# Expert rows scaled by slot and scatter-added to x1 in DRAM, with eight scan units after the last expert tile

## What is computed

```
x1  = x  + attention(layernorm(x), ctx)
x2  = x1 + moe16(layernorm(x1))          # 16 experts of width 192, top 2 per token, SiLU
x3  = x2 + mamba(ctx, layernorm(x2))     # state-space scan over 512 positions, 16 states, 512 channels
out = x3 + moe8(layernorm(x3))           # 2 of 8 experts of width 2048, GELU, chosen for all tokens
```

## Time and profile before

| | |
|---|---|
| time, median of 3 runs | 1595.75 us (1594.79 to 1597.31) |
| the profiled execution, first to last instruction | 1594.7 us |
| the median less that span | 1.05 us |
| PE busy, share of the span | 1391.5 us, 87% |
| DVE | 936.9 us, 59% |
| ACT | 709.8 us, 45% |
| POOL | 784.0 us, 49% |

### The profile page before, as it was taken

One profiled execution on the slowest core, in us unless ns is written; L12 is line 12 of the kernel. 1 busy time (PEld: TensorE's weight loads), 2 busy tenths in 40 slices (PEclk: granted clock), 3 DMA queues, 4 the chain that ended last, 5 costly groups with the idle time before them and its releaser, 6 DMA issues.

```text
span 1594.7 us, 18873 instructions
## 1 busy us (share of the span) xinstructions
PE 1391.5 (87%) x6080; PEld 1030.4 (65%) x6080; DVE 936.9 (59%) x1186; ACT 709.8 (45%) x1303; POOL 784.0 (49%) x607
## 2 busy tenths in 40 slices
PE   6988983588899989897166999999999999999998
PEld 3535532566666656664166787878787887878786
DVE  2677767999999999998683224241414224241413
ACT  4445433266766776665143333333333333333332
POOL 0000000788888988885631445444544545444442
PEclk9898895699999999999555999999999999999999
DMA  3202214477977987863655900010000100010000
GB/s 105 108 26 81 107 53 165 158 240 257 315 257 234 319 269 264 281 198 125 218 198 203 364 14 0 0 66 1 14 0 13 52 13 0 0 53 0 0 0 26
DMA packets 78202, 191.29 MB, mean 120 GB/s; under 512 B 10856, under 2 KB 15752, under 8 KB 77120
## 3 DMA queue, kind: packets, MB, share of 16 engines
q1 hardware_dynamic: 64832, 157.03, 29.3%
q0 software_dynamic: 6400, 20.98, 4.1%
q10 hardware_dynamic: 6912, 12.59, 2.2%
HBM read 152.55 MB, written 38.01 MB: 119 GB/s over the span
## 4 chain that ended last, share of the span: by engine, by line
PE 58%; DVE 22%; issue 10%; ACT 4%; POOL 3%; DMA 3%; ACTq 0%; SPq 0%; DVEq 0%; POOLq 0%
PE decay L1675 22%; PE bank L1664 21%; DVE decay L1247 11%; DVE S L1256 4%; PE bank L1474 2%; PE decay L1430 2%; PE bank L1437 1%; DVE XH L1114 1%; PE bank L1494 1%; PE bank L1534 1%; PE decay L1484 1%; PE bank L1619 1%; POOL Y L767 1%; PE bank L1561 1%; PE decay L1480 1%
## 5 line engine op out<-in xcount | busy, mean ns | idle before, releaser
L1387 DVE CAST HFH<-HF 128x512 fp32r<-128x512 f32 x128 | 59.0, 461 | 496.7 <-ACT HF L1045 496.7
L815 POOL TENSOR_TENSOR W2L<-W2R,W2H 128x512 fp32r<-128x512 f32 x128 | 172.5, 1347 | 348.2 <-ACT W2H L1040 348.2
L728 POOL TENSOR_TENSOR S<-DTU,Bb 128x1024 f32<-128x1024 f32 x128 | 304.7, 2401 | 25.1 <-DVE row_hot L1229 21.7
L1247 DVE TENSOR_TENSOR_SCAN decay<-decay,S 128x1024 f32<-128x1024 f32 x128 | 292.9, 2288 | 0.5 <-ACT decay L892 0.5
L1664 PE MATMUL bank<-XSH,W1H 128*128 128x512 f32 x512 | 202.9, 396 | 4.2 <-POOL W1L L811 4.2
L1675 PE MATMUL decay<-W2H,HFH 128*128 128x512 f32 x512 | 200.4, 391 | 5.3 <-DVE HFL L1389 5.3
L1664 PE MATMUL bank<-XSH,W1L 128*128 128x512 f32 x512 | 203.0, 396 | 0.0
L1664 PE MATMUL bank<-XSL,W1H 128*128 128x512 f32 x512 | 202.3, 395 | 0.0
L1675 PE MATMUL decay<-W2L,HFH 128*128 128x512 f32 x512 | 199.9, 390 | 0.0
L1675 PE MATMUL decay<-W2H,HFL 128*128 128x512 f32 x512 | 199.7, 390 | 0.0
L811 POOL TENSOR_TENSOR W1L<-W1R,W1H 128x512 fp32r<-128x512 f32 x128 | 171.1, 1337 | 49.6 <-ACT W1H L1031 49.6
(11 more groups left out here) (212 smaller groups left out, 2102.3 us busy)
## 6 DMA issues: line engine op xcount, KB each, us to landing
WGU<-in_L_ffn_gate_w SPq DMA_DIRECT2D x48, 384.0 KB, 3.8
WGU<-in_L_ffn_up_w SPq DMA_DIRECT2D x48, 384.0 KB, 5.1
WD<-in_L_ffn_down_w SPq DMA_DIRECT2D x48, 384.0 KB, 4.9
Bb<-bc_rows SPq DMA_DIRECT2D x32, 512.0 KB, 7.9
Cb<-bc_rows SPq DMA_DIRECT2D x32, 512.0 KB, 9.7
expert_rows<-YT ACTq DMA_DIRECT2D x48, 256.0 KB, 4.2
W1R<-in_L_ffn_w SPq DMA_DIRECT2D x6, 1024.0 KB, 13.9
W2R<-in_L_ffn_w SPq DMA_DIRECT2D x6, 1024.0 KB, 14.1
```

The lines of the kernel that those rows point to most:

```text
L728: pool.tensor_tensor(S[u % NP][:], DTU[:, ds(b, 1), c, :].to_broadcast([P, PAIR, L]), Bb[j][:], ALU.mult).then_inc(dbu_ready, 1)
L815: pool.tensor_tensor(W2L[f % 2][:], W2R[:, ds(e, 1), f, :].rearrange("p e d -> p (e d)"), W2H[f % 2][:].bitcast(F32), ALU.subtract).then_i ...
L1247: dve.tensor_tensor_scan(flat, flat, S[u % NP][:].rearrange("p i l -> p (i l)"), 0.0, ALU.mult, ALU.add).then_inc(scan_done, 1)
```

## The change

- The table by tile gets a second half: for each of the 32 pairs (choice k, token column) there are now two instructions of 48 elements, one with the token number plus 1, one with the routing weight. The contraction on TensorE has 96 columns in place of 48. VectorE then makes `slot_w` (half the weight of the slot), `slot_tok` and `slot_dst` (the token, or one of 128 spare rows where a slot is empty).
- `x1` is stored to `x2_rows` in DRAM. `copy_y` scales by the slot's weight into one of two `YT` buffers, and GpSimd adds the 128 rows onto `x2_rows` by an indirect DMA with an addition (`add_rows`). Each of these waits for the landing of the one before. ScalarE's store, all `gather_y`, `load_x1`, `add_first`, `add_second` and the copy to `gcol` are gone.
- 112 units are dealt over the tiles, and eight (`TAIL`) follow the last tile. The last two `add_rows` stand between these.
- SP loads `x2` for all four batches when the last addition has landed; X2 has four buffers. Three of the eight C buffers are loaded only after the routing, because the new table lies in their place.

```diff
-PAD = 6200
+PAD = 14200
+TAIL = 8
+LATE = 5
...
-        cuts = [AHEAD + (ALL - AHEAD) * j // SLOT_TILES for j in range(SLOT_TILES + 1)]
+        cuts = [AHEAD + (ALL - AHEAD - TAIL) * j // SLOT_TILES for j in range(SLOT_TILES + 1)] + [ALL]
...
-            sp.wait_ge(yt_stored, SLOT_TILES * DMA + DMA)
+            sp.wait_ge(yt_added, SLOT_TILES * DMA)
             sp.sem_inc(xt3_stored, DMA)
-            load_x1(0)
-            load_x1(1)
+            for b in range(B):
+                load_x2(b)
...
                 pool.wait_ge(xgt_ready, j + 1)
-                pool.tensor_copy(gcol[n % 2][:], slot_tok[:, ds(j, 1)]).then_inc(gcol_ready, 1)
-                wait_apart(pool, gcol_ready, j + 1)
                 pool.indirect_dma_start(out=XG[n % 2][:], out_offset=None, in_=xn_dram,
...
+            def add_rows(j):
+
+                pool.wait_ge(yt_ready, j + 2)
+                if j:
+                    pool.wait_ge(yt_added, j * DMA)
+                pool.indirect_dma_start(out=x2_rows, out_offset=bass.IndirectOffsetOnAxis(ap=slot_dst[:, j:j + 1], axis=0),
+                                        in_=YT[j % 2][:], in_offset=None, compute_op=ALU.add).then_inc(yt_added, DMA)
...
                 gate_by_up(j)
+                if j >= 2:
+                    add_rows(j - 2)
                 if j + 2 < SLOT_TILES:
                     gather(0, j + 2)
...
+            last = units(SLOT_TILES)
+            for u in last[:2]:
+                dbu(*bu(u))
+            add_rows(SLOT_TILES - 2)
+            dbu(*bu(last[2]))
+            add_rows(SLOT_TILES - 1)
+            for u in last[3:]:
+                dbu(*bu(u))
...
             for k in range(TOP):
-                ins = dve.tensor_tensor(
-                    tile_hot[:, k], iota_j[:].rearrange("p (o j) -> p o j", o=1).to_broadcast([P, NT, SLOT_TILES]),
-                    jf[:, k, :].rearrange("p (t o) -> p t o", o=1).to_broadcast([P, NT, SLOT_TILES]), ALU.is_equal)
-            do(ins)
-            for k in range(TOP):
-                dve.tensor_tensor(
-                    tile_hot[:, k], tile_hot[:, k], tokid[:].rearrange("p (t o) -> p t o", o=1).to_broadcast([P, NT, SLOT_TILES]),
-                    ALU.mult).then_inc(hot_ready, 1)
+                for t in range(NT):
+                    dve.tensor_scalar(tile_hot[:, k, t, 0, :], iota_j[:], jf[:, k, t:t + 1], tokid[:, t:t + 1],
+                                      ALU.is_equal, ALU.mult)
+                    ins = dve.tensor_scalar(tile_hot[:, k, t, 1, :], iota_j[:], jf[:, k, t:t + 1], rwt[:, k, t:t + 1],
+                                            ALU.is_equal, ALU.mult)
+            ins.then_inc(hot_ready, 1)
+            do(dve.tensor_scalar(spare_row[:], tokid[:, 0:1], float(B * L - 1), None, ALU.add))
...
-                    dve.tensor_copy(slot_tok[:], TURN[:, 0:SLOT_TILES]).then_inc(slots_ready, 1)
+                    ids = TURN[:, 0:SLOT_TILES]
+                    dve.tensor_scalar(slot_w[:], TURN[:, SLOT_TILES:2 * SLOT_TILES], 0.5, None, ALU.mult)
+                    dve.tensor_scalar(empty[:], ids, 0.0, spare_row[:], ALU.is_equal, ALU.mult)
+                    do(dve.tensor_scalar(tokf[:], ids, -1.0, 0.0, ALU.add, ALU.max))
+                    dve.tensor_copy(slot_tok[:], tokf[:])
+                    do(dve.tensor_tensor(empty[:], empty[:], tokf[:], ALU.add))
+                    dve.tensor_copy(slot_dst[:], empty[:]).then_inc(slots_ready, 1)
...
-            add_first(0)
-            add_second(0)
-            add_first(1)
+            for u in units(SLOT_TILES):
+                scan(*bu(u))
+                read_out(*bu(u))
+            statistics_x2(0)
+            statistics_x2(1)
```

More of the change, by code:

```diff
@@ L240, in build_program @@
         XT3 = sb(g, "XT3", [P, K, L])
+        logits = sb(g, "logits", [P, NT, E2])
         vare3 = sb(g, "vare3", [P, T])
@@ L366, in build_program @@
         yt_ready = sem("yt_ready")
[L367 to L373, removed]
+        yt_added = sem("yt_added")
+        spare_set = sem("spare_set")
+        x2_loaded = [sem(f"x2_loaded{b}") for b in range(B)]
         var2_ready = sem("var2_ready")
@@ L453, in build_program @@
         ALL = B * UB
-        cuts = [AHEAD + (ALL - AHEAD) * j // SLOT_TILES for j in range(SLOT_TILES + 1)]
+        cuts = [AHEAD + (ALL - AHEAD - TAIL) * j // SLOT_TILES for j in range(SLOT_TILES + 1)] + [ALL]
+        assert TAIL <= UB // 2
         def units(j):
-            return list(range(HP, AHEAD)) if j < 0 else list(range(cuts[j], cuts[j + 1])) if j < SLOT_TILES else []
+            return list(range(HP, AHEAD)) if j < 0 else list(range(cuts[j], cuts[j + 1])) if j <= SLOT_TILES else []
         def split(j):
@@ L502, in sequence_transfers @@
                     load_x(b + 1)
[L503 removed]
+                sp.dma_start(x2_rows[ds(b * L, L), :].rearrange("(t p) d -> p t d", p=P), X1A[:]).then_inc(x1_stored, DMA)
                 sp.wait_ge(xd_copied, b + 1)
@@ L510, in _ @@
             load_x(0)
+            sp.dma_start(x2_rows[B * L:B * L + P, :], x[0, 0:P, :]).then_inc(spare_set, DMA)
             for stored in (u_spilled, bc_stored, x1_stored, xn1_stored):
@@ L587, in _ @@
             load_down(0)
+            for j in range(LATE, NP):
+                load_c(0, j)
             load_gate_up(1)
@@ L951, in _ @@
             act.sem_inc(yt_ready, 1)
-            act.sem_inc(yt_stored, DMA)
             copy_xg(0, 0)
@@ L980, in _ @@
             copy_y(0, SLOT_TILES - 1)
-            store_y(0, SLOT_TILES - 1)
-            for u in units(SLOT_TILES - 2)[-1:] + units(SLOT_TILES - 1):
-                if u % HP == HP - 1:
-                    take(u)
+            before = units(SLOT_TILES - 2)[-1:] + units(SLOT_TILES - 1)
+            for u in units(SLOT_TILES):
+                if u != units(SLOT_TILES)[0]:
+                    decay(*bu(u))
+                for v in before:
+                    if v % HP == HP - 1:
+                        take(v)
+                before = [u]
+            take(ALL - 1)
             def silu_z(b):
@@ L1603, in _ @@
                 down(0, j)
-            for u in units(SLOT_TILES - 1):
+            for u in units(SLOT_TILES - 1) + units(SLOT_TILES):
                 add_states(*bu(u))
```

138 lines of the change are left out of this document (47 added, 91 removed).

## The result

The changed kernel takes 1643.6 us (median of four runs, 1638.5 to 1648.0), the kernel before 1595.3 us: a ratio of 1.030, 95% interval 1.0277 to 1.0322. That is 48.3 us slower where 11.8 were forecast, inside the range given (1583 to 1665). The direction and the table were right, the loop was not.

A forecast was written before the change was run, and what follows sets the result against it. It took VectorE to bound the loop, a chain of dependent steps the combine, TensorE the last stage. 20.7 + 1.1 + 23.0 - 33.0 = +11.8 us on a span of 1594.7, plus 1.05, gave 1607.6 us; range 1583 to 1665.

The forecast's parts named there:

- The table by tile, +20.7: Ahead of the first scan: VectorE's short table instructions and GpSimd's units shut each other out, 30.7 us in place of 10.0.
- The rival with a quick table: Ahead of the first scan: tensor_scalars run beside GpSimd, table +3.0 instead of +20.7, 1589.9 us; chance 0.22.
- Contraction and slot columns, +1.1: Behind the table: 96 columns cost TensorE nothing, six small VectorE instructions replace one CAST, +1.1 us.
- Loop and tail, +23.0: Eight units behind the last tile cost +27.8 us; 48 tiles at 8.85 for 8.95 us gain 4.8.
- the addition's issue 1.01 (taken as the gather's): In GpSimd's tile in the loop: issuing the addition was priced like a gather's issue, 1.01 us.
- the choice of 8.85 over 8.69: Loop: GpSimd's own work is 8.69 us a tile; with some waits for GU and landings, 8.85 was taken.
- the 8.37: Loop: tile time in us if VectorE went on setting the pace; rival that GpSimd keeps up, 1584.6 us, chance 0.08.
- the 0 of that case: Loop and tail: their cost if VectorE set the pace, 27.8 us gained in the loop against 27.8 in the tail.
- The combine, -33.0: From last read-out to last logits: SiLU sooner -17.3, gating sooner -7.7, batches closer together -8.0 us.
- Additions slow to land: Rival in the loop: each addition waits for the one before to land, 10 to 11.4 us a tile, 1663 to 1730; chance 0.18.

The follow-up runs named there:

- 1: The changed kernel, but GpSimd starts its eight units only when the table by tile is written: median 1633.9 us.
- number 3: The changed kernel with the rows scattered over x2_rows without adding (compute_op=ALU.add left out; wrong results): median 1616.8 us.
- number 4: The changed kernel without the additions, the indirect DMA replaced by an increment of its semaphore (wrong results): median 1589.5 us.
- number 7: The changed kernel with wide table and GpSimd behind it, gather at the tile's head, product on VectorE with both operands in SBUF: missed 1579 to 1586 by nearly 60 us.

## Why the prediction was wrong, point by point

- *The table by tile, +20.7.* Right: 9.8 to 30.5, +20.6, and shown by 1. The rival with a quick table is out.
- *Contraction and slot columns, +1.1.* Right: 323.72 to 324.69 us, +1.0.
- *Loop and tail, +23.0.* The step that failed: +64.0 (65.0 less the 1.0). The sentence "the addition's issue 1.01 (taken as the gather's)" is the one: 1.60 us. By number 3, which issues in 1.03, that is worth 22.9 of the 41 missing. The second term that was too small is the waiting, 0.16 us a tile in the choice of 8.85 over 8.69. Measured are 0.48, though the forecast had GpSimd's wait for GU near nothing. In the terms of the sum a tile of 9.57 us for 8.85 is 34.6 of the 41 us: 9.09 of GpSimd's own work for 8.69 is 19, the waits are 15. The tail adds 4.0; 2.4 are not placed. A gather issued behind an addition lands when TensorE already waits for it (59.3 us), GU comes late for GpSimd, and VectorE waits; moving the gather gave back 11.8. In the tail VectorE waits twice, 4.0 us in all, for `decay` on ScalarE, which stands in order behind a copy (`DTU`) that waits for TensorE; the forecast had the tail without a wait:

```profile
805.71 2.30 DVE L1235 TENSOR_TENSOR_SCAN decay<-decay,S 128x1024 f32<-128x1024 f32 x1 [1.76 <-ACT decay L883]
...
821.87 2.30 DVE L1235 TENSOR_TENSOR_SCAN decay<-decay,S 128x1024 f32<-128x1024 f32 x1 [2.21 <-ACT decay L883]
```

  That GpSimd takes VectorE's place as the limit was right, and by number 4 so is the 8.37 if it did not (there the stretch was still 7 us above the 0 of that case).
- *The combine, -33.0.* Right in mechanism, 4 us short: -37.3. SiLU comes 5.3 us behind the last read-out (5.2 forecast), gating 3.9 behind it (4.2), the normalisation 9.5 behind that (10.1); two batches take 26.7 (30.1); the last two 24.1 (24.2). Nearly all of the 3.4 us is batch 1, from its normalisation at 865.91 to the next at 877.74: 11.8 us, where TensorE's granted clock rose (0.71 from 867 to 875 us, 0.50 ahead of it) and runs of four transposes took 0.63 us and not 1.09. The kernel before had this too: its batch 1 took 9.2 us from normalisation (812.61) to logits (821.78) for the others' 12.1. The forecast priced all batches by the last two.
- *Additions slow to land.* False: they land in 6.0 us like a gather, and GpSimd waited 8.9 us for them in all. What they cost, they cost at their issue. With the addition they land in 6.0 us, without it in 5.1; less the issue that is 4.4 and 4.1 us, where this rival had it double. The Trainium skill's halved rate of a reducing DMA (page "Collectives: The Full Stack", section "The bandwidth ceiling: the fold count and why AG ≠ RS ≠ AR"), which the page gives for reduce-scatter on a ring, is not to be seen in that.

With GpSimd's tile as measured (3.65 + 2.333 x 2.33 = 9.09) and 0.48 for the waits the same sum gives 9.57 us a tile and 1607.6 + 34.6 = 1642 us.

## What to carry to other kernels

Where an engine has 0.9 us of slack in a tile of 9, price each instruction that is put on it from a row of its own kind; an indirect DMA with an addition is not a gather. Take its place in the order too: what is issued behind it comes later by its whole length, and what waits for that may be on another engine. And before moving work off GpSimd to VectorE, see where its operands are: a small product with both in SBUF cost 4.8 us in the median (1.8 on the mean in number 7), with one in PSUM 0.36.

## What the runs showed that I had not expected

- The issue of an indirect DMA on GpSimd: 0.99 us for a gather of 128 rows of 2 KB, 1.03 for a scatter, 1.60 for a scatter with addition.
- 64 short tensor_scalars get through between GpSimd's units one by one, but a tensor_tensor of 192 elements that came after a semaphore's release stood through two or three units in a row (up to 7.6 us). What decides between the two I did not try.
- 64 products with 96 columns took 10.6 us where with 48 they took 13.9. The granted clock differs: before it is 0.50 (1.2 GHz) all through, in the changed kernel 0.50 up to 314.5 us and 0.84 on the mean behind it. TensorE had sat idle for 25 us ahead of it before, for 45 us in the changed kernel. Why the clock rose in one and not in the other no run shows.
